# Gated cross-attention and feed-forward: where the products with V stand on TensorE, and which eviction comes first

## The reference

```
q = layernorm(x) @ Wq ; k, v = ctx @ Wk, ctx @ Wv       # 32 heads of 32, 8 key/value heads
P = softmax(q k^T / sqrt(32))                            # per head
x = x + tanh(g_xattn) * ((P v) @ Wo)
x = x + tanh(g_ffn) * ((silu(xn @ Wg^T) * (xn @ Wu^T)) @ Wd^T),  xn = layernorm(x), F = 2752
```

## Time and profile before

| | |
|---|---|
| Three runs | 1986.13, 1988.09, 1988.57 us; median 1988.09 |
| The profiled execution | 1986.94 us, its span 1984.7 us |
| PE busy | 1946.1 us, 98% of the span |
| DVE, ACT, POOL busy | 1256.0, 888.4, 902.0 us |
| Mean granted TensorE clock | 0.996 |
| Attention steps of a group | about 90 us each, four times |

### The profile page before, as it was taken

One profiled execution on the slowest core, in us unless ns is written; L12 is line 12 of the kernel. 1 busy time (PEld: TensorE's weight loads), 2 busy tenths in 40 slices (PEclk: granted clock), 3 DMA queues, 4 the chain that ended last, 5 costly groups with the idle time before them and its releaser, 6 DMA issues.

```text
span 1984.7 us, 28265 instructions
## 1 busy us (share of the span) xinstructions
PE 1946.1 (98%) x9568; PEld 1635.5 (82%) x9568; DVE 1256.0 (63%) x1766; ACT 888.4 (45%) x2109; POOL 902.0 (45%) x768
## 2 busy tenths in 40 slices
PE   7999999999999999999999899999999999999999
PEld 6888888888888888888888778878888888887887
DVE  7777776776887775555555367675555555536565
ACT  4883684487378353333333244443333333324333
POOL 2440342144145658888888510213667576540000
PEclk9999999999999999999999999999999999999999
DMA  5216325423424235545444676663323223248665
GB/s 203 83 60 221 93 59 192 124 71 125 163 76 151 96 112 180 181 146 180 157 170 146 247 262 223 208 214 121 106 98 114 87 98 126 85 145 295 197 217 190
DMA packets 125953, 298.84 MB, mean 151 GB/s; under 512 B 12704, under 2 KB 21920, under 8 KB 120480
## 3 DMA queue, kind: packets, MB, share of 16 engines
q1 hardware_dynamic: 125568, 297.06, 44.0%
q10 hardware_dynamic: 288, 0.52, 0.1%
HBM read 221.25 MB, written 71.57 MB: 148 GB/s over the span
## 4 chain that ended last, share of the span: by engine, by line
PE 82%; DVE 7%; ACT 4%; DMA 3%; POOL 2%; issue 1%; SPq 0%; POOLq 0%; ACTq 0%; DVEq 0%
PE ps L1636 26%; PE ps L1637 26%; PE ps L1638 26%; ACT pb L940 2%; PE ps L1686 2%; PE ps L1678 1%; PE ps L1677 1%; DMA raw<-ws 1%; DVE kb_h L1243 1%; DVE qo_l L1229 1%; DVE qo_h L1229 1%; DVE wc_l L1193 1%; PE ps L1851 1%; DVE bl L1193 1%; ACT wc_h L883 1%
## 5 line engine op out<-in xcount | busy, mean ns | idle before, releaser
L1636 PE MATMUL ps<-xop_h,w_h 128*128 128x512 f32 x1208 | 471.8, 391 | 0.0
L1638 PE MATMUL ps<-xop_h,w_l 128*128 128x512 f32 x1208 | 470.1, 389 | 0.0
L1637 PE MATMUL ps<-xop_l,w_h 128*128 128x512 f32 x1208 | 469.9, 389 | 0.0
L1193 DVE TENSOR_TENSOR bl<-raw,bh 128x1024 fp32r<-128x1024 f32 x154 | 197.1, 1282 | 153.7 <-ACT bh L883 153.4
L883 ACT ACTIVATE bh<-raw 128x1024 fp32r<-128x1024 f32 x154 | 163.3, 1062 | 244.7 <-PE ps L1638 206.7
L1638 PEld LDWEIGHTS ps<-xop_h,w_l 128*128 128x128 f32 x1208 | 226.8, 188 | 47.2
L1636 PEld LDWEIGHTS ps<-xop_h,w_h 128*128 128x128 f32 x1208 | 226.8, 188 | 46.7 <-DVE cc L1443 0.3
L1637 PEld LDWEIGHTS ps<-xop_l,w_h 128*128 128x128 f32 x1208 | 226.9, 188 | 46.1
L1636 PE MATMUL ps<-bh 128*128 128x512 f32 x616 | 245.5, 398 | 14.9 <-DVE bl L1193 10.4
L1193 DVE TENSOR_TENSOR w_l<-fraw,w_h 128x512 fp32r<-128x512 f32 x130 | 136.0, 1047 | 185.8 <-ACT w_h L883 185.8
L1638 PE MATMUL ps<-bh,bl 128*128 128x512 f32 x616 | 242.4, 393 | 0.0
(11 more groups left out here) (166 smaller groups left out, 3906.1 us busy)
## 6 DMA issues: line engine op xcount, KB each, us to landing
fraw<-in_wf SPq DMA_DIRECT2D x42, 1024.0 KB, 5.2
raw<-hs SPq DMA_DIRECT2D x154, 256.0 KB, 2.8
hs<-hsum SPq DMA_DIRECT2D x22, 1280.0 KB, 5.8
raw<-ws SPq DMA_DIRECT2D x110, 256.0 KB, 3.1
wc_raw<-in_wc SPq DMA_DIRECT2D x44, 512.0 KB, 4.4
dw<-in_wd SPq DMA_DIRECT2D x11, 1024.0 KB, 7.8
hs<-hb SPq DMA_DIRECT2D x44, 256.0 KB, 2.1
raw<-in_wd SPq DMA_DIRECT2D x44, 256.0 KB, 3.8
```

Of the source, the lines that this page charges most:

```text
L1193: return nc.vector.tensor_tensor(out, whole, hi.bitcast(F32), ALU.subtract)
L1636: pe.matmul(out, w_hi_, m_h, start=first, stop=False, skip_group_check=goes_on)
L1637: pe.matmul(out, w_hi_, m_l, start=False, stop=False, skip_group_check=goes_on)
L1638: return pe.matmul(out, w_lo_, m_h, start=False, stop=last, skip_group_check=goes_on)
```

## The change

On PE, `weigh_values(m)` moves from the end of step 2m + 6 to step 2m + 7, right behind that step's `scores`; the last one (m = 15) stays at the end of step 36. On ACT and on DVE, `pt_out` and `o_out` of a step change places.

```diff
 # ACT, body
                 for n in range(STEPS + 1):
+                    if 3 <= n < UNITS + 3:
+                        pt_out(g, n - 3)
                     if n >= 7 and n % 2 == 1:
                         o_out(g, (n - 7) // 2)
-                    if 3 <= n < UNITS + 3:
-                        pt_out(g, n - 3)
                     if n < UNITS:
                         exps(g, n)
 # DVE, body
-                    if n >= 7 and n % 2 == 1:
-                        m = (n - 7) // 2
-                        o_out(g, m)
                     if 3 <= n < UNITS + 3:
                         pt_out(g, n - 3)
+                    if n >= 7 and n % 2 == 1:
+                        o_out(g, (n - 7) // 2)
 # PE, body
                     if n < UNITS:
                         scores(g, n)
+                    if n >= 7 and n % 2 == 1:
+                        weigh_values(g, (n - 7) // 2)
                     if n < UNITS - 10:
                         q_part(n + 2)
...
-                    if n >= 6 and n % 2 == 0:
+                    if n == STEPS - 1:
                         weigh_values(g, (n - 6) // 2)
```

## The result

The changed kernel runs in 1996.94 us (median of six, 1992.91 to 1998.01) against 1987.68 for the one before (median of six, the three runs above among them): ratio 1.0043, 95% interval 1.0033 to 1.0053, so 8.5 us slower (6.6 to 10.5). The forecast was 1995.0 us, from a sum of 7.4 us. The profiled execution took 1998.01 us, its span is 1995.8.

The account below looks back on a forecast made before the run. PE was taken as the bound, busy 1946.1 of 1984.7 us. Terms of 0 + 0.5 + 0.3 + 1.05 = 1.85 us a group, 7.4 over four, gave 1995.5 from the median, stated as 1995.0; range 1989.5 to 2000.5.

Parts of the forecast that it names:

- Steps 7 to 9: Attention, P x V of pair 1 behind scores(9): the old wait is paid under another name, cost 0.
- Steps 9 to 21: Attention, pairs 3, 5 and 7: a new wait of 0.17 us at each, 0.5 us a group.
- Steps 21 to 25: New waits at first o_part (1.16), scores(25) (0.1 to 0.6), pair 9's P x V (0.6) outweigh 1.42; 0.3 us a group.
- Steps 30 to 33: End of attention: weigh_values(13) starts 1.05 us later behind scores(31) and swapped evictions, and nothing gives it back.
- PE's idle time: PE idle in a group's 90 us of attention: about 4.1 us in place of 2.2.
- Rival A: Scores in front cover the qo_l wait, swaps fall where ACT and DVE have room: 4 us faster, 1984; chance 0.08.
- C: A wait at every pair, 0.32 us lost at up to 15 pairs of four groups: 2007 us; chance 0.05.
- D: New waits drop PE's clock to 1.2 GHz, stretches behind eight long waits take twice as long: 2020 us; chance 0.02.
- The rule on DVE's pipe: DVE's next operation waits for an empty pipe: swaps cost 0.69, not 0.60, sum 1.8 us higher; forecast kept 0.60.

## Why the prediction was right

Sign, mechanism and place of every wait were right; the sum was 7.4 us for a measured 8.5 (6.6 to 10.5), 9.1 by the marks. No term came right by offsetting another: each of the four was forecast a little too low. The sum gave 1995.5 from the median; the last 0.5 was taken off without a reason.

- *Steps 7 to 9, forecast 0.* 0.1 in two groups, 0.3 in two. The new wait took the old one's place as forecast. The 0.2 between groups does not go with the change: DVE's query part starts 19.98 us after the group's first `scores` in the earlier trace rows and 20.18 after it in the changed kernel's group 1, and both values occur in groups of the experiments too. Where both kernels have the same value, 20.2 in group 0 and 20.0 in group 3, the change costs 0.1. The later start goes with group 0 of the kernel before waiting 0.54 and not 0.32. Why a group enters attention with ACT and DVE 0.2 later or earlier I haven't tested.
- *Steps 9 to 21, forecast 0.5.* 0.62, three times 0.21 in place of 0.17. At pair 3 it is a start that comes 0.15 us late and a term that I had left out: the first matmul behind a wait takes longer, 0.35 us at 259.42 against 0.28 at 309.58, and its successor starts 0.07 later. The view of waits lists nothing here, since the modelled end of the matmul in front, 259.15 + 0.28, already reaches the late start; only distances and marks show it. That the two swaps are needed together is shown by the runs with one of them.
- *Steps 21 to 25, forecast 0.3.* 0.37. The waits came where they were forecast and are listed with 0.83, 0.28 and 0.41 us against 1.16, 0.1 to 0.6 and 0.6. As delays of starts they are nearer: the first `o_part` begins 1.99 us after `scores(22)`, and 0.92 before, so 1.07 late; P x V of pair 9 begins 1.14 after `scores(25)` and not 0.56, so 0.58 late. The prediction's own times give 0.50 for the latter, 292.76 against 291.70 + 0.56, and not the 0.6 that it names; its 0.3 a group does not rest on that figure. The statement that mattered, that the wait at `o_part` is nearly all given back, is shown by its removal, which gains nothing.
- *Steps 30 to 33, forecast 1.05.* 1.07, link by link. It was the largest term and the surest one.
- *PE's idle time.* The forecast was 4.1 us a group in place of 2.2; between the marks it is 3.42. The time lost was added to the idle time as if the profile showed all of it, and half of it lies where the profile shows a matmul still running.
- *Rival A* came near the gain of PE's move: -0.75 us a group, and -0.95 in group 0, where DVE's query part starts alike in both; it had said -1.0. What it got wrong is the price of the swaps, as its own condition (0.56 against 0.88) had it. *C*: the pairs up to 11 whose eviction stands behind no query part did not wait, in no run. *D*: the clock stayed at 1.00 through waits of 1.49 us and behind them. The prediction argued against D from waits of up to 1.3 us, although its own chain made pair 13 wait about 1.5, longer than the 1.42 that the earlier trace rows cover. That the clock would hold there too was not shown before the run.
- *The rule on DVE's pipe.* In the changed kernel `pt_l` of 0.69 us at 245.95 is followed at 246.56, so after 0.61, and the sum by the row was the better one at every link of the last stretch. The prediction told only half of the rule that it cited. The Trainium skill ("VectorE: DVE Perf Modes", section "The DRAIN you can't avoid") has the next operation wait for the pipe to empty, but adds that "a next op that is not held starts earlier", with no figure. The trace agrees with that addition: in the rows of steps 7 to 9 the second instruction of the query part, 0.69 us from 245.23, is followed after 0.72, behind its end, and `pt_out` after 0.61, before its end.

The profiled execution of the changed kernel lies 11.1 us above that of before, of which 9.55 are there at the last P x V. The other 1.5 lie behind it, in the rest of the output projection and the feed-forward layer, which are the same in both. The profiled execution is the slowest of the changed kernel's six runs. I don't count the 1.5 to the change; what they come from is not shown.

## What to carry to other kernels

Where an engine's queue is an order written by hand, an eviction costs nothing as long as it fills a slot in which its engine waits anyway; put behind the next, longer eviction, it inherits that one's wait, and on two engines in a row the delays add up until they exceed the slack of whoever reads the result. A wait in the profile is not its price: take the time between marks at which both kernels have done the same work, since a wait that appears can be one that has only moved, and a loss can be too short to be listed (here the listed idle time grew by half of the time lost). When a wait is due to a loaded stretch of a helper engine, move that engine's deferrable work (here a weight split) into a step in which it idles, and fill what remains with the bound engine's own work from elsewhere.

## What the runs showed of the hardware

The first matmul of 256 columns behind a listed wait takes 0.35 to 0.39 us in place of 0.28, and its successor starts 0.19 to 0.23 us behind it in place of 0.12; behind transposes it is 0.36 (P x V at 267.88). DVE's evictions kept their durations in all twelve kernels: `pt_out` 0.65 to 0.69 us, `o_out` 0.39 to 0.43. In 76 to 120 of the 128 `pt_out` of each kernel the instruction behind it started 0.58 to 0.61 us after it, so before its end. Behind the second instruction of a query part the next never started before its end, at the earliest 0.72 us after its start (32 cases in each kernel).
